# Layer 0 of a two-layer sequence block: the transposed input loaded instead of made, modulation in row tiles, keys and queries ahead of the cross matmuls

## The reference

```python
# layer 0, x is (32, 128, 128): batch, time t, channel c
ctx   = causal_ema(x, tau_ctx)
wg    = sigmoid([x, ctx] @ Wg.T + bg);  gated = x * wg
h1    = gelu(x @ Wn1.T + bn1)                       # 32 hidden
mod   = 0.5 + sigmoid(h1 @ Wn2.T + bn2)             # 32 decay channels
traces   = causal_ema(gated * mod[..., d], tau[d])  # for each of 32 d
temporal = sum over d of traces * softmax(blend)[d]
gate  = sigmoid(temporal @ Wtemp.T + btemp)
soma  = gelu(x @ Wsoma.T + bsoma)
x     = x + layernorm((soma * gate) @ Wout.T)
...
# layer 1: attention with 16 heads of 8, dense or sparse by row; x + attention(x)
```

## Time and profile before

| what | value |
|---|---|
| median of 3 runs | 373.5 us (368.14 to 380.67) |
| profiled execution | 366.06 us, its span 364.3 us |
| front, to 29.45 us | span 29.45 us |
| step 0, to 59.66 us | 30.21 us |
| step 1, to 80.37 us | 20.71 us |
| steps 2 to 6, to 181.50 us | 20.29, 20.07, 20.26, 20.26, 20.25 us |
| `end` and attention | the other 182.8 us |
| busy over the span | PE 86%, DVE 82%, POOL 65%, ACT 59% |
| mean granted clock | 0.959 |

### The profile page before, as it was taken

One profiled execution on the slowest core, in us unless ns is written; L12 is line 12 of the kernel. 1 busy time (PEld: TensorE's weight loads), 2 busy tenths in 40 slices (PEclk: granted clock), 3 DMA queues, 4 the chain that ended last, 5 costly groups with the idle time before them and its releaser, 6 DMA issues. The chain is left out here.

```text
span 364.3 us, 10344 instructions
## 1 busy us (share of the span) xinstructions
PE 311.9 (86%) x3351; PEld 213.7 (59%) x3361; DVE 296.9 (82%) x1530; ACT 213.2 (59%) x452; POOL 236.9 (65%) x281
## 2 busy tenths in 40 slices
PE   1769559998999989898938499899899989999994
PEld 0425227565564746564524466777687768777772
DVE  4775997979797878879784877799799989999971
ACT  5833201565646364554705367787688868888772
POOL 2045143464655566564733497699899999999980
PEclk9969788999999999999978989999999999999998
DMA  7101000101001035100552004425544564454011
GB/s 206 48 0 31 0 0 2 30 4 29 2 0 31 3 87 94 20 0 0 74 70 32 0 4 86 91 62 71 141 102 98 82 131 104 98 78 103 3 31 30
DMA packets 23473, 18.91 MB, mean 52 GB/s; under 512 B 2304, under 2 KB 23040, under 8 KB 23424
## 3 DMA queue, kind: packets, MB, share of 16 engines
q1 hardware_dynamic: 23424, 18.31, 25.0%
HBM read 3.62 MB, written 2.10 MB: 16 GB/s over the span
## 5 line engine op out<-in xcount | busy, mean ns | idle before, releaser
L1411 POOL TENSOR_TENSOR arena<-arena,neg_max 128x512 f32<-128x512 f32 x128 | 130.1, 1050 | 21.5 <-DVE neg_max L1285 21.2
L1285 DVE CUSTOM_DVE_ANT_0 arena<-ps,arena 128x128 f32<-128x128 f32 x512 | 113.8, 286 | 13.4 <-PE ps L655 7.5
L934 ACT ACTIVATE arena<-ps 128x512 f32<-128x512 f32 x128 | 69.7, 596 | 16.3 <-PE ps L669 16.3
L669 PE MATMUL ps<-ident_sb,arena 128*128 128x128 f32 x512 | 69.1, 279 | 0.0
L1371 POOL TENSOR_TENSOR arena<-arena 128x448 f32<-128x448 f32 (+6 forms) x56 | 41.8, 746 | 29.9 <-DVE arena L1113 27.4
L669 PEld LDWEIGHTS ps<-ident_sb,arena 128*128 128x128 f32 x512 | 57.0, 142 | 6.6 <-issue 4.2
L1358 POOL TENSOR_TENSOR arena<-decay_a,arena 128x192 f32<-128x192 f32 x32 | 22.3, 717 | 38.5 <-ACT arena L794 38.5
L1285 DVE DVE_READ_ACCUMULATOR2_ANT neg_max<- 128x1 f32 x512 | 42.5, 83 | 0.0
L685 PE MATMUL ps<-arena 128*32 128x128 f32 x1024 | 41.5, 280 | 0.0
L1113 DVE TENSOR_TENSOR arena<-ps,arena 128x448 f32<-128x448 f32 (+6 forms) x56 | 23.5, 426 | 14.2 <-PE ps L456 8.7
L655 PE MATMUL ps<-arena 48*128 48x128 bf16 x512 | 25.7, 220 | 8.3 <-DVE neg_max L1285 5.7
(11 more groups left out here) (154 smaller groups left out, 594.5 us busy)
## 6 DMA issues: line engine op xcount, KB each, us to landing
arena<-q_parts SPq DMA_DIRECT2D x96, 64.0 KB
arena<-k_parts SPq DMA_DIRECT2D x96, 64.0 KB
arena<-in_x SPq DMA_DIRECT2D x8, 256.0 KB, 2.8
out<-arena SPq DMA_DIRECT2D x8, 256.0 KB, 3.0
w_sb<-in_w SPq DMA_DIRECT2D x1, 576.0 KB, 6.5
arena<-in_consts SPq DMA_DIRECT2D x1, 420.0 KB, 5.5
rows_sb<-in_rows SPq DMA_DIRECT2D x1, 288.5 KB, 3.0
ident_sb<-in_ident SPq DMA_DIRECT2D x1, 64.0 KB, 3.1
```

The source lines that it names most:

```text
L669: mm = pe.transpose(ps[1][:, q % 2, k * P:k * P + P], neg_t[q % NT_RING][:, k * P:k * P + P], ident)
L934: act.activation(probT[q % PT_RING], ps[1][:, q % 2, :], ACT.Exp, scale=-1.0)\
L1285: dve.tensor_tensor_reduce(out=neg_t[q % NT_RING][:, cs], in0=ps[0][:, score_bank(c) + slot, cs], in1=nbias[n % 2], scale=1.0, scalar=3.0e ...
L1411: pool.tensor_tensor(t4, t4, neg_max[:, n % 2, 4 * z:4 * z + 4].unsqueeze(2).broadcast_to([P, 4, P]), ALU.subtract).then_inc(s["shifted"], 1)
```

## The change

It does four things. The input transposed on the host (`xt`) is a new argument, loaded straight into `xT`; the transposes of `f_x` on PE and the copy on ScalarE are gone. Its transfer for group n waits until the cross matmuls of group n - 2 have read the same memory. The modulation matmuls use 32 rows of the array each, in two halves of two with a gate matmul between them, and write to columns of banks 0 and 1; `wn2_row` and its set-up on VectorE are gone. On PE, `f_soma` and `f_hidden` stand ahead of the carries, and keys, then queries, ahead of `b_cross`. On VectorE the modulation tensors (`f_modulation`) are made before `f_gated`, and the splitting of them (`f_mod_parts`) after the locals. `end` has keys before queries.

```diff
-            def f_x(i, m):
+            def f_context(i, m):
...
                 pe.wait_ge(s[f"x_loaded{u}"], i * 16 + 16 * (m // 2 + 1))
                 if not at_start(i, m, 2):
 
                     pe.wait_ge(s["temporal_ready"], grp(i, m, 1, -1))
-                turned(bank(u, 0), xn[u], "xT_ps")
...
+            def f_modulation(i, m, half):
+
+                u = m % 2
+                if half == 0:
+                    pe.wait_ge(s["h1_ready"], grp(i, m, 1, 1))
+                    pe.wait_ge(s["ctx_ready"], grp(i, m, 1, 1))
+                    pe.wait_ge(s["soma_ready"], grp(i, m, 1, 1))
...
+                else:
+                    pe.wait_ge(s["modT_half"], grp(i, m, 1, 1))
+                for k in range(2):
+                    b = 2 * half + k
+                    rows_of = slice(b * D, b * D + D)
+                    mm = pe.matmul(mod_banks(u)[:, k, half * P:half * P + P], wn2_sb[rows_of, :],
+                                   h1T[u][rows_of, :], start=True, stop=True)
+                mm.then_inc(s[("modT_half", "modT_ps")[half]], 1)
...
             def step(i, m):
-                f_x(i, m + 1)
+                closes = not at_start(i, m, 1)
                 f_context(i, m + 1)
+                f_soma(i, m + 1)
+                f_hidden(i, m + 1)
                 b_carries(i, m)
-                f_soma(i, m + 1)
-                f_gate(i, m + 1)
-                f_hidden(i, m + 1)
+                f_modulation(i, m + 1, 0)
+                f_gate_x(i, m + 1)
+                f_modulation(i, m + 1, 1)
+                f_gate_ctx(i, m + 1)
                 b_locals(i, m)
-                f_modulation(i, m + 1)
-                if not at_start(i, m, 1):
+                if closes:
                     c_x1T(i, m - 1)
+                f_modulation_n(i, m + 1)
                 f_gated(i, m + 1)
+                if closes:
+                    c_k(i, m - 1)
+                    c_q(i, m - 1)
                 b_cross(i, m)
...
+                sp.wait_ge(s["cross_ps"], grp(i, m, 1, -1))
+                sp.dma_start(by_row(xT[m % 2]), xt[:, group_rows(i, m), :]).then_inc(s[f"xT_loaded{m % 2}"], 16)
```

More of the change, by code:

```diff
@@ L80, in scal, with build @@
     return ACT_STEPS.index(name) + 1
-def build(nc, x, w, wn2, cols, rows, consts, ident_in, idx, masks, out):
+def build(nc, x, xt, w, wn2, cols, rows, consts, ident_in, idx, masks, out):
     with ExitStack() as ctx:
@@ L237, in build, with mod_banks @@
         block = ctx.enter_context(nc.Block())
+        def mod_banks(u):
+            return ps[u][:, 0:2, 0:2 * P]
         def at_start(i, m, before):
@@ L412, in f_hidden @@
                 mm.then_inc(s["h1_ps"], 1)
-            def f_modulation(i, m):
+            def f_modulation(i, m, half):
                 u = m % 2
-                pe.wait_ge(s["h1_ready"], grp(i, m, 1, 1))
-                if at_start(i, m, 1):
-                    pe.wait_ge(s["vec_step"], vec(f"wn2_row{GB - 1}"))
-                for b in range(GB):
-                    mm = pe.matmul(bank(u, 1)[:, b * P:b * P + P], wn2_row[:, b, :], h1T[u], start=True, stop=True)
-                mm.then_inc(s["modT_ps"], 1)
+                if half == 0:
+                    pe.wait_ge(s["h1_ready"], grp(i, m, 1, 1))
+                    pe.wait_ge(s["ctx_ready"], grp(i, m, 1, 1))
+                    pe.wait_ge(s["soma_ready"], grp(i, m, 1, 1))
+                    if at_start(i, m, 1):
+                        pe.wait_ge(s["wn2_loaded"], 16)
+                else:
[6 more added lines that the diff above has]
+                mm.then_inc(s[("modT_half", "modT_ps")[half]], 1)
             def f_modulation_n(i, m):
@@ L531, in c_x1T, with c_k @@
                 turned(closing_bank(i, m, 3), x1g[u], "x1T_ps")
+            def c_k(i, m):
+                pe.wait_ge(s["x1T_ready"], grp(i, m, 1, 1))
+                pe.matmul(closing_bank(i, m, 3), wt["wk"], x1T, start=True, stop=True).then_inc(s["k_ps"], 1)
             def c_q(i, m):
@@ L570, in front @@
                 f_hidden(i, m)
-                f_gate(i, m)
-                f_modulation(i, m)
+                f_modulation(i, m, 0)
+                f_gate_x(i, m)
+                f_modulation(i, m, 1)
+                f_gate_ctx(i, m)
                 f_modulation_n(i, m)
@@ L788, in f_modulation @@
                 act.wait_ge(s["modT_ps"], grp(i, m, 1, 1))
-                act.activation(thd[u], bank(u, 1), ACT.Tanh, bias=hb[:, 2:3], scale=0.5).then_inc(s["modT_tanh"], 1)
+                act.activation(thd[u].rearrange("p (c k t) -> p k c t", c=2, k=2),
+                               mod_banks(u).rearrange("p k (c t) -> p k c t", c=2), ACT.Tanh, bias=hb[:, 2:3],
+                               scale=0.5).then_inc(s["modT_tanh"], 1)
             def f_modulation_n(i, m):
@@ L824, in c_part @@
             def c_part(i, m, n, part):
-                done, ready = ((("q_ps", "k_ps")[n], "part1_ready"), ("rest1_ps", "part2_ready"),
-                               ("rest2_ps", "part3_ready"))[part]
-                act.wait_ge(s[done], grp(i, m, 2, n + 1) if part else grp(i, m, 1, 1))
+                qk = "qk"[n]
+                done = (f"{qk}_ps", f"{qk}_rest1_ps", f"{qk}_rest2_ps")[part]
+                ready = (f"{qk}_part1_ready", f"{qk}_part2_ready", "part3_ready")[part]
+                act.wait_ge(s[done], grp(i, m, 1, 1))
                 act.activation((q_parts, k_parts)[n][:, part, group_cols(i, m)], closing_bank(i, m, 2 + n), ACT.Identity,
@@ L832, in c_parts @@
             def c_parts(i, m, part):
+                c_part(i, m, 1, part)
                 c_part(i, m, 0, part)
-                c_part(i, m, 1, part)
             def front(i, m):
-                f_x(i, m)
                 act.wait_ge(s["const_loaded"], 16)
@@ L1002, in _ @@
             pro("k_bias", dve.tensor_copy(hb[:, 4:5], col["bk"]))
-            dve.wait_ge(s["wn2_loaded"], 16)
-            for b in range(GB):
-                rows_of = slice(b * D, b * D + D)
-                pro(f"wn2_row{b}", dve.tensor_copy(wn2_row[rows_of, b, :], wn2_sb[rows_of, :]), waited=b == GB - 1)
             dve.wait_ge(s["act_step"], scal("softplus"))
@@ L1195, in front @@
             def front(i, m):
+                f_modulation(i, m)
                 f_gated(i, m)
[L1197 removed]
+                f_mod_parts(i, m)
                 f_lags(i, m, range(Q))
@@ L1438, in _ @@
             over_octets(octet_step)
-_ORDER = ["x", "w", "wn2", "cols", "rows", "consts", "ident", "idx", "masks"]
+_ORDER = ["x", "xt", "w", "wn2", "cols", "rows", "consts", "ident", "idx", "masks"]
 def shape_constants():
```

103 lines of the change are left out of this document (49 added, 54 removed).

## The result

| | kernel before | changed kernel | ratio, 95% interval |
|---|---|---|---|
| first comparison, median | 377.03 us (368.14 to 380.67) | 382.73 us (379.74 to 387.84) | 1.037 (1.023 to 1.051) |
| second comparison | 370.4 us (369.79 to 371.74) | 378.22 us (377.09 to 382.55) | 1.022 (1.016 to 1.028) |
| profiled execution | 366.06 us | 380.86 us (second: 377.09) | |
| start of the first score matmuls of `end` | 181.62 us | 188.11 us (second: 187.23) | |

A forecast was written before the change was run, and what follows sets the result against it. The step was taken as a loop through PE and VectorE in three legs. Steps 2 to 6 add 12.9 us, step 1 +1.1, step 0 +0.7: +14.7 us on 366.06 us gives 380.8 us, range 372 to 398.

The forecast's parts named there:

- its other base, the median: The three runs' median of the kernel before, 373.5 us; with the 14.7 us added the forecast is 388.2 us.
- Third, and the largest: GpSimd gets in between: GpSimd's additions take the SBUF port twice, ahead of the second modulation instruction and the gated input on VectorE: +2.05 us a step.
- rival 2: Nobody waits for the port: +2.4 us, 375.9 us, or 368 if the hidden matmuls did not wait either; chance 0.20.
- the sum: Steady step: -1.63 + 1.5 + 0.65 + 2.05 = +2.6 us, so about 22.8 us; in all +14.7 us.
- The third leg: Cross matmuls to the end of lag 6, 10.34 us on PE; 1.63 us a step saved, with 0.56 us idle at crossT.
- The first term: Hidden matmuls ahead of the carries wait on PE for the centring, so VectorE's carries start later: +1.5 us a step.
- The second term: VectorE's modulation pair, formerly behind the locals under the cross, now stands ahead of the locals: +0.65 us a step.
- The second leg: End of the centring to the cross matmuls: 6.49 us, on VectorE without a gap; work added there is paid in full.
- vanish in the same waits: Tiling-mode drains on PE, if 0.1 us at each of four changes, would disappear in PE's waits for VectorE.
- Front, step 0 and step 1: Layer 0's beginning: 0 for front, +0.7 us for step 0, +1.1 us for step 1.
- The transfers: Loads of xT, x and the stack have time to land before they are needed; cost none.
- Rival 4: New PE idle ahead of the gated transposes lowers the clock: some 2.2 us more a step, up to 401 us; chance 0.15.

The follow-up runs named there:

- second comparison: The changed kernel timed once more with no edit, against the kernel before: 378.22 us against 370.4 us, ratio 1.022 (1.016 to 1.028).

## Why the prediction was right and wrong

Right is the verdict, slower, and the time of the profiled execution, 380.86 us for 380.8 us. That agreement is chance. By its other base, the median, the prediction gave 388.2 us against 382.73 us, and its rivals' times stand on that base, so its 380.8 us can't be set beside their 381.9 and 375.9 us. The forecast put 14.7 us into layer 0; 6.5 us are there (5.6 us in the second trace), and the rest lies in an attention that was 8 us longer in this execution.

**What failed: "Third, and the largest: GpSimd gets in between".** 2.05 us a step, 12.3 us in all, measured 0. The pair and the gated input kept their durations, and GpSimd waited. The mechanism is real: with the same three instructions it cost 2.15 us when each waited for the end of the one ahead, and 0.76 us a step when VectorE stood for ScalarE ahead of them. What the prediction took from the earlier trace rows was that GpSimd gets in at the first boundary; in this place it did not, and why not is open. By mechanism rival 2 was the case (nobody on VectorE waits); its +2.4 us fell short of the 5.6 to 6.5 us by what the sum lacked (below).

**The third leg, -1.63 us:** -1.45 us. crossT waited 0.72 us where 0.56 us was forecast. Right.

**The first term, hidden ahead of the carries:** PE's wait 1.05 us for 1.3 us, the carries 1.62 us behind the centring for 1.57 us. The mechanism was read rightly. "Paid in full" was wrong: with the carries ahead again the step got longer, and without the collision 0.46 us shorter. So its price in this place was 0.5 us in place of 1.5 us. The modulation, whose chain begins at hidden, had been put ahead of the locals as well, so the chain from hidden over ScalarE to VectorE's pair sets nearly the same time.

**The second term, +0.65 us:** the pair takes 0.67 us there. But taking it away made VectorE wait for the tanh and let GpSimd in, so its own price stays unmeasured.

**What the sum lacked.** Without the port it gives steps of 20.8 us; they are 21.6 us. The second leg was costed on VectorE alone, and PE had become its bound: 0.28 us a step are the queries ahead of the cross, of which the prediction counted only what they took from the third leg, 0.34 us are the row tiles, which the prediction let "vanish in the same waits" that the change itself had filled. Both were measured, each by itself; since the parts don't add when turned round together, this is no full account. By legs, the second is 0.72 us longer than the sum without the port, the third 0.18 us longer, the first 0.08 us shorter.

**Front, step 0 and step 1** were forecast at 0, +0.7 and +1.1 us and came at -0.8 (second trace -0.7), +0.3 (second trace -0.7) and -0.3 us. **The transfers** cost nothing, as said. **Rival 4**, the clock: 1.00 in the steady steps, so not the case; in steps 2 to 5 it occurred only in the experiment in which PE stood 1.84 to 1.85 us ahead of the gated transposes, and there in every other step.

GpSimd's 2.23 us against 1.57 us agree with the rule of the Trainium skill, "SBUF — State Buffer", section "Who interferes with whom", that 2-port work of VectorE and work with two inputs in SBUF exclude GpSimd from the shared ports. The same section of the Trainium skill also says who wins: "Whoever issues first gets the shared pair for the whole instruction". By the starts of the rows, the collisions of the experiments fit it: in step 4 of each, GpSimd's row begins 0.25 to 0.35 us ahead of the VectorE row that takes 1.26 to 1.63 us. The changed kernel does not fit: GpSimd's row begins 0.07 us ahead of L1103 and 0.41 us ahead of the gated input, and both kept their durations. Who gets the ports decided 12 us of the forecast.

## What to carry to other kernels

Filling a hole in one engine's row with moved work pays only up to the length of the hole, its own waits counted: 0.39 us and one matmul pair fitted into 1.17 us and gave 0.47 us a step, two pairs gave nothing. When several things are moved onto one stretch, cost that stretch again on every engine; the one that waited before (PE here) may have become the one that is waited for, and then small things such as tile modes count. And a stall price seen at one place is a price, not a probability. Here it was paid wherever VectorE came to a halt at or between the instructions, and once without a halt, so the same instructions have to be run at the new place before the price is added up by steps.

## What the runs showed of the hardware

- GpSimd's additions came ahead of VectorE's SBUF instructions where VectorE stood for ScalarE (1.26 us for 0.42 us, 1.52 us for 0.68 us) or for the end of its own instruction just ahead (1.38 and 1.63 us for 0.42 and 0.68 us). In both traces of the changed kernel they did not (0.42, 0.42, 0.68 us), though the gated input had a semaphore to wait for there too, one already met. Following without a wait does not keep GpSimd out either: L1103 took 1.49 us with the carries ahead of hidden, and the second one-hot of the earlier trace rows 1.11 us. What decides is open.
- A half of the modulation (two matmuls of 128 columns) in row tiles took 0.42 us from start to start, at full height 0.45 us. A full matmul between row-tiled ones took 1.06 us, with a row-tiled one only behind it 0.95 us, between full ones 0.86 us.
- With PE's wait at 1.85 us the clock fell (0.57 over the next 3.8 us) in steps 2, 4 and 6 of one run; with 1.91 us in step 1 and 1.84 us in steps 3 and 5 it stayed at 1.00. The length of the wait alone does not decide it.
